# Waits on TensorE's counts ahead of row gathers, against a memset ahead of each gather, in a two-layer graph attention kernel

## Reference

```python
edge_index = jnp.stack([src, dst])
h = jnp.maximum(_layernorm(x, axis=-1), 0.0)
x = x + _L0_gnn_ref(h, L0_gnn_W, L0_gnn_att, L0_gnn_bias, edge_index)
h = jnp.maximum(_layernorm(x, axis=-1), 0.0)
x = x + _L1_gnn_ref(h, edge_index, edge_attr_32, L1_gnn_Wq, ...)
```

## Time and profile before

| | us |
|---|---|
| median of 3 runs | 1561.81 (1560.83 to 1562.72) |
| span of the profiled execution | 1585.9 |
| POOL busy (926 instructions) | 883.4, 56% |
| PE busy (4985) | 1020.5, 64% |
| DVE busy (3002) | 934.6, 59% |
| ACT busy (1699) | 640.0, 40% |

### The profile page before, as it was taken

How to read it: one execution, slowest core, us unless ns; L and a number is a source line. 1 busy time by engine, 2 the same in 40 slices (tenths; PEclk the granted TensorE clock), 3 DMA queues, 4 the chain that set the end, 5 groups by cost and what they waited for, 6 DMA issues and landing times.

```text
span 1585.9 us, 21105 instructions
## 1 busy us (share of the span) xinstructions
PE 1020.5 (64%) x4985; PEld 863.7 (54%) x4985; DVE 934.6 (59%) x3002; ACT 640.0 (40%) x1699; POOL 883.4 (56%) x926
## 2 busy tenths in 40 slices
PE   5456666666665766666554577666766676676765
PEld 4345555555554555445354466565655566566664
DVE  6445656556565565557813455656565656656578
ACT  5524334243342433422554234444443434344414
POOL 5766666666666566551046566656666565666500
PEclk9655555555656565566766666877777777777676
DMA  6321222222222222222133222222222222232201
GB/s 138 72 66 43 66 46 66 48 63 45 67 47 67 45 65 47 58 84 57 49 94 95 73 84 84 84 80 80 84 84 84 80 82 81 84 88 83 80 1 41
DMA packets 54202, 110.35 MB, mean 70 GB/s; under 512 B 16876, under 2 KB 30848, under 8 KB 53956
## 3 DMA queue, kind: packets, MB, share of 16 engines
q0 software_dynamic: 36288, 91.12, 22.6%
q1 hardware_dynamic: 16483, 17.39, 4.0%
q10 hardware_dynamic: 1313, 0.50, 0.1%
HBM read 100.60 MB, written 8.81 MB: 69 GB/s over the span
## 4 chain that ended last, share of the span: by engine, by line
DVE 16%; PE 16%; another core or an unknown queue 10%; issue 9%; ACT 2%; DVEq 2%
PE bank L865 6%; PE bank L849 6%; DVE acc L1441 4%; DVE PV L1418 3%; DVE prod L1238 2%; PE bank L836 1%; PE bank L912 1%; DVE raw L1247 1%; DVE halves L1087 1%; PE bank L900 1%; DVEq L1441 1%; ACT S L636 1%; DVEq L1220 0%; DVEq L90 0%
## 5 line engine op out<-in xcount | busy, mean ns | idle before, releaser
L532 POOL DMA_INDIRECT G<-table,idx_all x880 | 857.1, 974 | 544.5 <-issue 280.3
L865 PE MATMUL bank<-PV,S 128*125 128x144 f32 x1760 | 449.5, 416 | 209.5 <-DVE acc L1441 104.4
L865 PEld LDWEIGHTS bank<-PV,S 128*125 128x125 f32 x1760 | 373.9, 287 | 236.1 <-issue 134.9
L1441 DVE TENSOR_TENSOR acc<-acc,bank 125x144 f32 x880 | 260.4, 296 | 339.3 <-remote 191.7
L636 ACT ACTIVATE S<-iota_n,lid 128x125 f32<-128x125 f32 x880 | 275.7, 386 | 0.7 <-issue 0.7
L849 PE MATMUL bank<-qe,ST 125*128 x880 | 182.0, 378 | 87.3 <-DVE prod L1238 80.7
L849 PEld LDWEIGHTS bank<-qe,ST 125*128 125x128 f32 x880 | 164.1, 279 | 96.7 <-issue 95.8
L1418 DVE TENSOR_TENSOR PV<-G,PV 128x512 f32<-128x512 f32 x220 | 151.2, 688 | 23.4 <-issue 22.8
L646 ACT ACTIVATE ST<-bank 125x512 f32<-125x512 f32 x110 | 63.6, 598 | 248.4 <-remote 197.6
L640 ACT ACTIVATE S<-S,ones 128x500 f32<-128x500 f32 x220 | 156.6, 712 | 7.3
L836 PE MATMUL bank<-ident,S 128*125 128x128 f32 x440 | 89.8, 340 | 52.5 <-ACT S L640 31.9
(11 more groups left out here) (219 smaller groups left out, 1093.8 us busy)
## 6 DMA issues: line engine op xcount, KB each, us to landing
G<-table,idx_all POOLq DMA_INDIRECT x880
prod<-in_edge_attr_dram SPq DMA_DIRECT2D x8, 672.0 KB
table<-G SPq DMA_DIRECT2D x12, 224.0 KB
bias_rows<-qe SPq DMA_DIRECT2D x1, 1664.0 KB
table<-h0b SPq DMA_DIRECT2D x8, 178.5 KB
out_dram<-G SPq DMA_DIRECT2D x8, 168.0 KB
prod<-in_edge_attr_dram SPq DMA_DIRECT2D x8, 90.0 KB
xs<-in_x_dram SPq DMA_DIRECT2D x1, 504.0 KB
```

Of the source, the lines that this page charges most:

```text
L532: pool.indirect_dma_start(G[:, u, v, 0:w], None, table, bass.IndirectOffsetOnAxis(ap=idx_all[:, g * GV + v:g * GV + v + 1], axis=0)).then_ ...
L865: last = pe.matmul(sums_bank(p)[0:BN, at:at + H * SLOT], S[:, ur, v, :], PV[:, v, :, :].rearrange("p h k -> p (h k)"), start=True, stop=True)
L1441: ve.tensor_tensor(a, a, o, ALU.add).then_inc(s.sem["acc_added"], 1)
```

## The change

`pace` and its call go. In its place stands `space`: GpSimd writes zeros into `w0n` (128 partitions x 128 floats), the first layer's weights, which nobody reads any more at that time, and each such memset raises a count of its own. The next memset waits for the count of the one before, so that no two writes of `w0n` are open at once. The other waits of `gathers` stay.

```diff
+        s_space = sem("spacer_set")
...
-            def pace(n, g, v):
-
-                s, r, q = L[n], g - UNROLL, g - 1
-                if v % 4:
-                    return
-                if g == 0:
-                    if v == 12 and n == 0:
-                        wait(pool, s["t_done"], 4)
-                    return
-                if n == 0:
-                    if v == 0:
-                        wait(pool, s["expanded"], 4 * q + 2)
-                        if r >= 0:
-                            wait(pool, s["mm_done"], NB * r + 3)
...
-                    if v == 8:
-                        wait(pool, s["scoreT"], g)
...
+            spaces = [0]
+
+            def space():
+
+                wait(pool, s_space, spaces[0])
+                pool.memset(w0n[:, :], 0.0).then_inc(s_space, 1)
+                spaces[0] += 1
...
                         for v in range(QV * j, QV * j + QV):
-                            pace(n, g, v)
+                            space()
                             pool.indirect_dma_start(
```

## The result

| us | before | after | ratio, 95% interval |
|---|---|---|---|
| forecast | | 1446 (1405 to 1640) | 0.926 |
| measured, medians of 4 runs each | 1562.26 | 1739.29 | 1.113 (1.109 to 1.117) |
| span of the profiled execution | 1585.9 | 1745.6 | |

The change makes the kernel 11% slower where 7% faster was forecast, and the time lies outside the range. It is the rival that the prediction called starved (1667 to 1777), which it had given 0.17.

A forecast was written before the change was run, and what follows sets the result against it. The prediction took PE's late counts, held behind a backlog of gathers, as the bound. At 1.44 us per gather the loops save 45.8 and 69.7: 1585.9 becomes 1470.4, the median 24.1 lower, 1446 us; range 1405 to 1640.

The forecast's parts named there:

- starved: Rival in both gather loops: backlog not cured, GpSimd runs until the ring stops it; 1667 to 1777 us, chance 0.17.
- What bounds the kernel: Both gather loops: no engine's work is the bound; PE's counts reach other engines late, stuck behind a backlog from close gathers.
- The 236 us: Removing GpSimd's two waits per step: up to 55 x 4.3 = 236 us less POOL waiting, only while the rest keeps up.
- The price of the memset: Memset before each gather: bounds 0, 0.15, 0.19, far above 0.35; took 0.19 us, making 1.44 us per gather.
- The interval of no backlog: Gather spacing in both loops: 0.13 to 0.15 us backlog per gather, so 1.39 us apart would leave none; 1.44 gives prompt counts.
- The sum: Both loops at 440 x 1.44 = 633.6 us: -45.8 and -69.7, so 1470.4 profiled and 1446 us median.
- The last term: Whole kernel: the median of the runs lies 24.1 us below the profiled execution, taking 1470.4 to 1446 us.
- its signs: Gathers 1.25 to 1.35 apart in runs of 12 and more, DVE's `pv_ready` waits, DVE idle "remote" over 8 us.
- Dear memset: Rival in both loops: at 1.60 us an interval +25, 1587 us; level at 1.57; chance 0.07 with about equal.
- cheaper than thought: Rival in both loops: interval 1.40 with prompt counts, 616 us each, -150.7, 1411 us; below 1405 had chance 0.03.
- prompt at 1.25: Case in both loops: counts prompt at 1.25 us spacing, 550 and 564 us, near 1293 us; no mechanism seen for it.
- Taken alone: Skill page's reading of PE's counts as prompt: holes stay, memsets add 880 x 0.19 = 167 us; given no chance of its own.

The follow-up runs named there:

- Bare3: Kernel before with the waits on PE's counts taken out and no memset put in, third run, late session: 1783.2 us, ratio 1.123.
- w256: Changed kernel with each memset writing 256 columns instead of 128, late session: 1615.2 us, ratio 1.018 to the kernel before.
- w288: Changed kernel with each memset writing 288 columns instead of 128: 1498.4 us, 1.116 in a prompt session; 1498.1 us, 0.958 in a late one.
- w288b: Repeat of the changed kernel with memsets of 288 columns instead of 128, prompt session: 1497.9 us.
- bare: Kernel before without waits on PE's counts and without memsets: 1343.6 us, 0.999 in a prompt session; 1783.2 us, 1.123 in a late one.
- bare2: Kernel before without waits on PE's counts and without memsets, second run, prompt session: 1344.1 us beside a before of 1346.1.
- after2: The changed kernel itself run again, unaltered, beside the kernel before in a prompt session: 1376.9 us, ratio 1.024.
- w288c: Repeat of the changed kernel with memsets of 288 columns instead of 128, late session: 1498.1 us, ratio 0.958 to the kernel before.
- two2: Changed kernel with two memsets of 144 columns before each gather instead of one of 128, late session: 1537.2 us, ratio 0.986.

## Why the prediction was wrong

**What bounds the kernel: right for a late session.** PE's counts reach the others late, and with the stops of GpSimd at `pace` the kernel loses less by it. Bare3 shows it from the other side: without the stops 12% more. The 236 us that the removal was to bring at most, "only while the rest keeps up", didn't come, since the rest did not keep up. What the rows of one trace couldn't tell is that there are sessions without any lateness; there the waits are worth nothing either way.

**The price of the memset: the first step that failed.** The prediction took 0.19 us on top of 1.25, the middle row being 0.15, and had argued that the 0.30 us belongs to the indirect DMA itself. It does so only between two indirect DMAs. Behind a memset the gather starts after 0.16, so the memset of 0.22 costs 0.08, and the interval is 1.33. The 0.08 lies halfway between the lower bound of 0 ("it runs inside the 0.30") and the middle one of 0.15, and the 0.19 of the sum is more than twice as much. With it, by the prediction's own 1.39, the forecast would have been the starved case.

**The interval of no backlog: the second, and the deeper one.** Had the price been right, the time would still have been missed: w256 has just the forecast's 1.44 us and takes 1615, not 1446. The 0.13 to 0.15 us for each gather were read rightly as how fast a backlog grows. With 1.39 a run of 16 at 1.334 should clear in 1.80 - 8 x 0.14 + 16 x 0.056 = 1.6 us, and it takes 1.76. But from "the backlog doesn't grow" I concluded "the counts are prompt", and at 1.44 they weren't: 679 us of "remote" waits, and a count 4.0 us late before the run's end. Rows 6 could have warned: there DVE idles 15.5 us for a count while the backlog is worth 3.6. One reading is that a count isn't held for as long as the backlog ahead of it lasts, but until a moment in which there is none, and that such moments are too rare at 1.44 and come at 1.47. It fits the rows of before, after and w256, but it was made after them and tested by none; no run shows the queue itself.

**The sum: right in form.** Where counts are prompt GpSimd is the bound and a time follows from the interval: for w288, 203 + 880 x 1.475 = 1501, measured span 1500.7 in the late session and 1496.1 in a prompt one (w288b). The last term, by which the median was to lie 24.1 us under the profiled span, was 6.3 for after (1745.6 against 1739.3).

**The rivals.** Starved decided "when the real interval is clearly under 1.39", and gave 27 to 29 us a step; measured 26.8 and 28.9, with 330 us of waits on `pv_ready`, gathers 1.33 apart and DVE idle "remote" for up to 9.7 us, all as its signs were written down. It should have had most of the chance, since prices of 0 to 0.14 lay under 1.39 and the rest rested on one row of the same shape. Dear memset (1.57 as the point of level) didn't come. Of cheaper than thought, "prompt at 1.25" did, though for bare in a prompt session and at 1344, not 1293: GpSimd has no hole in its loops there, but they take 573.6 and 567.5 us in bare2, where 550 and 564 had been put. Not all gathers take 0.94, as the prediction had it (one of the earlier trace rows takes 1.36; the mean of bare2 is 0.99), so the interval is 1.29 to 1.30 in the mean.

**The pages.** In the prompt sessions PE's count is used 0.04 us after its end (bare2, above), in the late ones DVE idled 15.51 us for one that was long there. The Trainium skill (Perfetto Trace Analysis, per-instruction lifecycle) has the count pushed when PSUM acknowledges the write. Taken alone, as the prediction took it, that makes every session prompt and the memsets a mere cost. Four of the seven sessions are of that kind, and the prediction had given it no chance.

The memset shows no sign of being held up by DVE's work: 220 ns in the mean of after's 880, 282 at most, against 194 for the same shape at the program's start. That is the 0.19 of the forecast within 0.03, and agrees with what the Trainium skill (SBUF — State Buffer, two separate sides) says of a GpSimd instruction that only writes.

The Trainium skill (DMA: Bandwidth & Descriptors, Why a DMA increments its semaphore by 16 and not by 1) says that for a DMA issued by GpSimd all 16 DMA engines post an increment of their own. That would be a candidate for what each gather adds to a common path; no run here varied it. The traces agree in a prompt session: bare2 has 16,014 records of DMA increments, of which 880 x 16 = 14,080 would be the gathers'.

**What stays open.** Why sessions come in two kinds. The kernel, the chip's number and the gathers' own duration (0.94 or 0.95 us in both) are the same. Two obvious causes don't fit. The DMA packets of the gathers' queue aren't slower: they take 19.0% of 1745.6 us in after (late), 332 us an engine, and 25.3% of 1374.2 in after2 (prompt), 348 us. Nor is PE: it is busy for 918 us of after's loops and 844 of after2's, 74 more, where the spans lie 371 apart.

One difference is plain. The late traces hold far fewer records of count updates: 8,832 in before, 9,757 in after, 9,196 in bare3 and 9,671 in w256, against 21,162 in bare2 and 22,023 in after2, though the same kernel makes the same updates. w288c has 12,988 and two2 15,290, against 22,083 and 22,959 in prompt sessions, so these two were late ones, whatever their time. It also means that the sums of "remote" waits in late traces are drawn from part of the records. Whether what writes these records is also what holds the counts back, so that the lateness would come with the measuring, no run here tested. Nor was anything tried by which a late session could be turned into a prompt one.

## What to carry to other kernels

A wait that guards nothing can still carry the time: before it is taken out, look at whether other engines' idle time ends in the hole that it makes. A filler instruction costs its interval, not its duration: read what it adds from where the next instruction starts, with fillers of two or three sizes. And a gain that hangs on how late counts arrive has to be measured in several sessions, side by side with the old kernel: here the same edit is 1.024 or 1.113, and a memset of 288 columns 1.116 or 0.958. Of the kernels tried none beats before in both kinds; w288 beats both kernels in late sessions (1498 against 1565 and 1739), and before stays the best in prompt ones.

## What was not expected of the hardware

- The two kinds of session: the same kernel in 1344 or in 1558 to 1586 us, with no wait "remote" in any trace or with 797 us of them in that of before, and nothing between; the late traces hold 8,832 to 15,290 records of count updates, the prompt ones 21,144 to 22,959.
- Between two indirect DMAs GpSimd idles 0.30 us, between a memset and an indirect DMA 0.16 (0.18 behind one of 8 columns), and none before the memset. A memset of 128 x 8 takes 124 ns and widens the interval by 0.01 us.
- The lateness of PE's counts in late sessions has an edge: with gathers 1.44 us apart 679 us of "remote" waits, at 1.47 32 us, at 1.50 none.
